# Second attention and expert rounds in one block: the norms of three token chunks in the attention's tail, the fourth within the first expert steps

## The chip, the cores and the metric

One NeuronCore of a Trainium2 chip runs the whole program in one launch. The metric is the device time of one execution in microseconds (us); lower is better. The engines are PE (TensorE, matmuls), DVE (VectorE), ACT (ScalarE), POOL (GpSimd) and SP (SyncE, which here only issues transfers). Each runs its own list of instructions in order and waits for the others through semaphores.

## What is computed

Two layers over 2 x 1024 tokens of 128 channels. The first (a rotary attention and a windowed transformer) is not touched. The second, cut to what matters here:

```python
h = causal_attention(norm(x))          # 16 heads of 8 channels, scores over 1024 tokens
h = layernorm(h_in + z) * gamma + beta # z: the heads' output, NaN taken as 0
x = x + g2 * h
cur = adaln(x)                         # layer norm, scale and shift by the condition
for r in range(4):                     # expert rounds
    w = top2_softmax(cur @ Wg[r] + bg[r])                # 4 experts, 2 kept
    cur = cur + sum_e w[e] * (gelu(cur @ W1[e] + b1[e]) @ W2[e] + b2[e])
x = x + g5 * cur
```

## The kernel before

Activations lie with channels on the partitions, tokens along the free dimension, in four **chunks** of 512 tokens. `causal_block` runs the second attention, then `heads_and_experts` runs everything behind it, each in a block of its own: at the end of a block all engines meet, and the semaphores are cleared.

**Second attention** (`attention`, L661 on). Eight units `it` (four heads of one batch each) of 16 **quarters** give `LAST` = 128 quarters `g`. In each quarter PE computes four score tiles (`score`, L835) into three PSUM banks, ACT turns each into probabilities with Exp (L925), and PE adds the values of the quarter before (`values`, L853, L856, L862). A score tile waits until ACT has emptied the bank of three tiles before. Besides, PE runs 11 quarters ahead with matmuls (L803) whose row maxima DVE reduces (L936), so that DVE has no maxima to reduce in the last 11 quarters. POOL multiplies the diagonal probabilities by a triangle (`mask`, L1020) in eight quarters of each unit, four and four. At a unit's end ACT copies the sums out of PSUM (`take_sums`, L911), PE transposes them (`turn`, L825), DVE divides (L955, L960) and SP stores the heads to DRAM (`store_z`, L761). What else is due in a quarter is listed by `entries(g)`, and PE works it off behind `values(g - 1)`.

**Heads and norms** (`heads_and_experts`, L1793 on). SP loads the heads back as rows of 128 channels (L1885), then the expert weights and small tables (L1886 to L1892). For each chunk: DVE's `compare` and `guard` (L2127, L2133) take NaN as 0, PE transposes (`turn`, L1916), DVE adds to `h` (L2138). Then follow two norms of class `ChunkNorm`, n3 and n4: PE averages over channels (L331), DVE subtracts (L336), ACT squares (L341), PE sums the squares (`variance`, L347), ACT takes the root (L353), DVE inverts (L358), PE spreads the inverse over the partitions (L364), DVE rescales (L370), ACT adds the shift (L375); between the norms DVE adds to x (`add_x`, L2142). The four chunks go through this as a pipeline of `PERIODS` = 8 written out by hand. POOL meanwhile splits both weight tensors into a high and a low part (L2099, L2102, L69), since every product of the experts is made of three matmuls (L74, L75, L76).

**Expert steps.** `STEPS` = 64 steps n, 16 a round: chunk n // 4 % 4, expert n % 4. A step is `up(n)` (12 matmuls), `activate(n)` on ACT (four Gelu, L2033, three copies, L2039), `cast_first` and `lower_hidden` on DVE (L64, L69), `lower_last` on POOL (L2094), `down(n)` (12 matmuls), `weigh(n)` on DVE (L2169) and `add_term` on POOL (L2089). PE issues `up(n + 1)` ahead of `down(n)`.

**Gates.** Each half of the tokens in each round has a gate g: `gate_logits` on PE (L1965), ranking on DVE (L2192 to L2221), `gate_exp` (L2044), `turn_weights` (L1971), `take_rows` (L2024), then SP stores the rows (L1898) and loads them spread over the partitions (L1904), which `weigh` of its eight steps waits for. `gate_after` places the parts: logits behind step 8g - 7, the turning in step 8g - 2, rows behind `activate(8g - 1)`. `weigh(0)` stands on DVE behind `cast_first(2)`.

```python
                for n in range(1, STEPS):
                    if n + 1 < STEPS:
                        up(n + 1)
                    if n == 1:
                        turn_weights(0)
                    g = gate_after(n - 5)
                    if g:
                        turn_weights(g)
                    down(n)
                    g = gate_after(n)
                    if g:
                        gate_logits(g)
```

## Time and profile before

| | us |
|---|---|
| three runs | 1779.31, 1780.4, 1783.44 |
| median | 1780.4 |
| the profiled execution | 1784.86 |
| its span in the trace | 1783.1 |
| PE busy in the span | 1555.6 (87%) |
| DVE busy | 1349.5 (76%) |
| ACT busy | 1193.9 (67%) |
| POOL busy | 623.2 (35%) |

The span starts with the first instruction and ends with the last; the profiled execution took 1.8 us more than its span and 4.5 us more than the median. The granted clock is a share of TensorE's 2.4 GHz: 1.00 is 2.4 GHz, 0.50 is 1.2 GHz. A row of the timeline gives the start and the duration of an instruction or of a merged run of equal ones (x4), the engine, the line, and in square brackets how long the engine had been idle before it and what released it.

### The profile page before, as it was taken

To read this page: it belongs to the slowest core of one execution; us is meant where nothing else is said; L and a number is where in the kernel's file an instruction comes from. 1 tells how busy PE (TensorE), PEld (TensorE's weight loads), DVE (VectorE), ACT (ScalarE), POOL (GpSimd) and SP (SyncE) were. 2 spreads that over 40 slices of the span, in tenths; PEclk is the share of its full clock that TensorE was granted. 3 is DMA by queue.
4 is the path that set the end of the run, shared out by engine and by line. 5 is a ranking of instruction groups with operands and counts; after the bars stand their busy time and mean duration, and the time that the engine had idled before them with its cause. 6 is when DMAs were issued, how large, how long until landed. Compare 5 with 4: busy or idle time off the path is not lost. (4 is left out here: it accounts for less than half of the span.)

```text
span 1783.1 us, 29420 instructions
## 1 busy us (share of the span) xinstructions
PE 1555.6 (87%) x11136; PEld 856.1 (48%) x11136; DVE 1349.5 (76%) x1876; ACT 1193.9 (67%) x2314; POOL 623.2 (35%) x510
## 2 busy tenths in 40 slices
PE   6699999996589886898985999999966799999998
PEld 4122222222457663576641233333324688878886
DVE  3799999981777456775446999999915499999996
ACT  4368888885377742777551787788763577787776
POOL 2710000000577542775230122222213255555554
PEclk9689999998599987999995899999997799999999
DMA  2320110001011100111003201110011111111111
GB/s 75 106 89 20 31 24 19 1 2 51 25 31 31 50 1 18 31 31 31 4 20 94 90 20 28 32 26 6 5 19 60 35 50 43 48 43 48 43 47 53
DMA packets 68284, 66.05 MB, mean 37 GB/s; under 512 B 40840, under 2 KB 44296, under 8 KB 67632
## 3 DMA queue, kind: packets, MB, share of 16 engines
q1 hardware_dynamic: 67504, 61.94, 13.1%
q8 instruction: 89, 1.46, 0.3%
q10 hardware_dynamic: 576, 2.16, 0.3%
q14 instruction: 51, 0.42, 0.1%
q0 software_dynamic: 64, 0.07, 0.0%
HBM read 40.85 MB, written 14.81 MB: 31 GB/s over the span
## 5 line engine op out<-in xcount | busy, mean ns | idle before, releaser
L936 DVE TENSOR_REDUCE att_neg_max<-psum 128x1 f32<-128x1024 f32 x512 | 600.6, 1218 | 46.8 <-PE psum L803 42.6
L925 ACT ACTIVATE att_probs<-psum 128x512 f32<-128x512 f32 x1024 | 532.3, 604 | 142.4 <-PE psum L835 139.9
L803 PE MATMUL psum<-att_k_op,att_q_op 48*128 48x512 bf16 x1024 | 339.2, 406 | 20.3 <-DVE att_neg_max L936 11.9
L835 PE MATMUL psum<-att_q_op,att_k_op 50*128 50x512 bf16 x1024 | 314.3, 387 | 25.2 <-ACT att_probs L925 25.1
L2033 ACT ACTIVATE moe_hidden<-psum,moe_b 128x512 f32<-128x512 f32 x256 | 167.4, 690 | 83.5 <-PE psum L76 83.3
L835 PEld LDWEIGHTS psum<-att_q_op,att_k_op 50*128 50x128 bf16 x1024 | 78.0, 94 | 272.7 <-ACT att_probs L925 218.3
L69 DVE TENSOR_TENSOR moe_hidden_low<-moe_hidden,moe_hidden_high 128x512 fp32r<-128x512 f32 x192 | 203.8, 1108 | 5.4 <-ACT moe_hidden_high L2039 5.3
L853 PE MATMUL psum<-att_probs,att_v 128*32 128x512 f32 (+2 forms) x1664 | 203.2, 558 | 2.9 <-ACT att_sums L911 2.8
L1020 POOL TENSOR_TENSOR att_diag<-att_probs,att_triangle 128x512 f32<-128x512 f32 x64 | 81.0, 1266 | 278.0 <-PE psum L856 172.6
L2094 POOL TENSOR_TENSOR moe_hidden_low<-moe_hidden,moe_hidden_high 128x512 fp32r<-128x512 f32 x64 | 93.6, 1462 | 169.7 <-ACT moe_hidden_high L2039 169.7
L803 PEld LDWEIGHTS psum<-att_k_op,att_q_op 48*128 48x128 bf16 x1024 | 73.7, 95 | 126.1 <-DVE att_neg_max L936 101.5
L1684 POOL TENSOR_TENSOR wl_qk<-wl_qk,wl_part 128x512 f32<-128x512 f32 x64 | 81.5, 1274 | 106.7 <-DVE wl_part L1563 106.7
L2089 POOL TENSOR_TENSOR moe_cur<-moe_cur,moe_term 128x512 f32<-128x512 f32 x64 | 105.8, 1652 | 14.0 <-DVE moe_term L2169 13.8
L74 PE MATMUL psum<-moe_hidden_high,moe_w_high 128*128 128x512 f32 x256 | 103.5, 404 | 5.6 <-DVE moe_hidden_low L69 5.6
L2039 ACT ACTIVATE moe_hidden_high<-moe_hidden 128x512 fp32r<-128x512 f32 x192 | 106.6, 625 | 0.0
L74 PE MATMUL psum<-moe_cur_high,moe_w_high 128*128 128x512 f32 x256 | 101.9, 398 | 0.0
L1580 DVE TENSOR_REDUCE wl_mx<-psum 128x4 f32<-128x512 f32 x64 | 44.0, 687 | 75.6 <-PE psum L1296 75.6
L76 PE MATMUL psum<-moe_hidden_high,moe_w_low 128*128 128x512 f32 x256 | 100.8, 394 | 0.0
L75 PE MATMUL psum<-moe_hidden_low,moe_w_high 128*128 128x512 f32 x256 | 100.8, 394 | 0.0
L76 PE MATMUL psum<-moe_cur_high,moe_w_low 128*128 128x512 f32 x256 | 100.2, 391 | 0.0
L75 PE MATMUL psum<-moe_cur_low,moe_w_high 128*128 128x512 f32 x256 | 100.1, 391 | 0.0
L1009 POOL COPY att_v<-v_tok 128x256 f32<-128x256 f32 x16 | 6.4, 400 | 248.6 <-PE psum L853 246.3
(254 smaller groups left out, 2851.5 us busy)
## 6 DMA issues: line engine op xcount, KB each, us to landing
moe_spread_weights<-gate_rows SPq DMA_DIRECT2D x64, 256.0 KB, 3.2
wl_v_shift<-wl_v SPq DMA_DIRECT2D x62, 128.0 KB, 2.2
att_q_op<-qk_parts SPq DMA_DIRECT2D x32, 192.0 KB, 3.3
att_k_op<-qk_parts SPq DMA_DIRECT2D x32, 192.0 KB, 4.3
qk_parts<-att_hi SPq DMA_DIRECT2D x12, 256.0 KB, 4.0
qk_parts<-att_hi SPq DMA_DIRECT2D x12, 192.0 KB, 2.9
att_q_op<-att_neg_rows SPq DMA_DIRECT2D x128, 2.0 KB
qk_parts<-att_mid SPq DMA_DIRECT2D x8, 256.0 KB, 3.2
```

Of the source, the lines that this page charges most:

```text
L69: return dve.tensor_tensor(dst, src, high.bitcast(F32), ALU.subtract)
L74: pe.matmul(out, w_high, x_high, start=start, stop=False)
L75: pe.matmul(out, w_high, x_low, start=False, stop=False)
L76: return pe.matmul(out, w_low, x_high, start=False, stop=stop)
L803: mm = pe.matmul(buf[:, half * CHUNK:(half + 1) * CHUNK], q_op[it % RING][at_rows(p, MAX_ROW), j, t * P:(t + 1) * P], k_op[it % RING][at_r ...
L835: pe.matmul(st_bank[e % 3], k_op[it % RING][at_rows(p, MAX_ROW + 2), j, t * P:(t + 1) * P], q_op[it % RING][at_rows(p, MAX_ROW + 2), j, ha ...
L853: last = pe.matmul(out[:, 0:full], stage_v[r][:, t, j, :], pr[:, 0:full], start=first_tile, stop=final and full == CHUNK, skip_group_check ...
L925: act.activation(probs[:, g % PB, h, :], st_bank[e % 3], ACT.Exp, scale=scale).then_inc(exp_done, 1)
L936: dve.tensor_reduce(neg[:, t, 2 * p + j:2 * p + j + 1], ring[e % 2], AX.X, ALU.max, negate=True).then_inc(ring_free, 1)
L2033: act.activation(hidden[:, n % 2, f, :], k.psum[:, f, :], ACT.Gelu_apprx_tanh, bias=b1[:, e, f:f + 1]).then_inc(gelu_done, 1)
L2039: act.activation(hidden_high[:, n % 2, f, :], hidden[:, n % 2, f, :], ACT.Copy)\
L2089: pool.tensor_tensor(cur[:, at], cur[:, at], term[:, n % 2, :], ALU.add).then_inc(added, 1)
```

## The change

The two blocks become one: `heads_and_experts` is called from `attention` and gives it pieces that each engine runs inside and behind the attention's own work. What it does:

- SP loads the weights behind the operands of unit 3, in unit 0, and the heads of chunks 0 to 2 in units 3, 5 and 7; those of chunk 3 behind the last store. There are four semaphores `z_stored`, one a chunk.
- POOL splits the weights in units 1 and 2, and clears `square` in unit 3, each behind the fourth mask.
- In the last ten quarters PE, ACT and DVE work off the transposing, n3, `add_x` and n4 up to the variance for chunks 0 to 2 (`tail_on_pe`, `tail_on_act`, `tail_on_dve`). The squares and the shifts of both norms move from ACT to DVE (`square_on_dve`, `add_shift_on_dve`).
- Behind the last `turn` follow n4's rescaling of chunks 0 to 2 and gate 0. Chunk 3 goes through its heads and both norms within steps 0 to 5; gate 1 (its logits need chunk 3) moves from step 1 to step 6, its turning from step 6 to step 8, its rows from behind `activate(7)` to behind `activate(9)`.
- `take_rows(0)` moves into `activate(3)`, `down(2)` waits for it, and `weigh(0)` stands behind `lower_hidden(2)`.
- `cur` takes the memory of `v_ch`, the raw weights that of `centred_x` and `square`; other tensors lie where the attention's were. The banks of the norms are 5, 6, 4, 6, and the last turn takes banks 0 and 1.

In the diff, the order is: the new pieces of `ChunkNorm`; `attention` on SP, PE, ACT, DVE and POOL; the placing of the gates; then the work in the tail and behind it on PE, ACT, POOL and DVE.

```diff
+    def square_on_dve(self, dve, c):
+        dve.wait_ge(self.centred, c + 1)
+        d = self.d[:, self.at[c]]
+        dve.tensor_tensor(self.sq[:, self.at[c]], d, d, ALU.mult).then_inc(self.squared, 1)
+    def add_shift_on_dve(self, dve, c):
+        dve.wait_ge(self.scaled, c + 1)
+        dve.tensor_scalar(self.dst[:, self.at[c]], self.d[:, self.at[c]], self.shift(c * CHUNK // SEQ), None, ALU.add)\
+           .then_inc(self.shifted, 1)
 ...
+                if behind and it == 0:
+                    then.load_weights(sp)
                 if causal and it:
                     store_z(it - 1)
+                if behind and it in (3, 5, 7):
+                    then.load_z(sp, it // 2 - 1)
             if causal:
                 store_z(UNITS - 1)
-                sp.wait_ge(z_stored, 16 * GROUP * UNITS)
+            if behind:
+                then.load_z(sp, CHUNKS - 1)
+                then.on_sp(sp)
 ...
                 extras(entries(g))
+                if behind:
+                    then.tail_on_pe(pe, g)
             values(LAST - 1)
+            if behind:
+                then.last_variance(pe)
             turn(UNITS - 1)
+            if behind:
+                then.on_pe(pe)
 ...
+                if behind:
+                    then.tail_on_act(act, g)
 ...
-            work(order[2 * CHUNKS:])
+            work(order[2 * CHUNKS:-1])
+            if behind:
+                then.tail_on_dve(dve)
+            turn(UNITS - 1)
+            if behind:
+                then.on_dve(dve)
 ...
                     for t in range(SEQ_TILES):
                         mask(it, t)
+                        if behind and t == 3:
+                            then.split_weights(pool, it)
 ...
+    def gate_at(n, first, later):
+        if n == first:
+            return 1
+        g = n // 8 + 1
+        return g if n % 8 == later and 2 <= g < GATES else None
 ...
+    banks = [5, 6, 4, 6]
+    OUT_BANKS = (5, 4, 7)
 ...
+    def tail_on_pe(pe, g):
+        left = own.quarters - g
+        if left == 10:
+            turn_z(pe, 0)
+        if left == 9:
+            turn_z(pe, 1)
+            average3(pe, 0)
+        if left == 8:
+            average3(pe, 1)
+            turn_z(pe, 2)
+        if left == 7:
+            n3.variance(pe, 0)
+            n3.variance(pe, 1)
+            average3(pe, 2)
+        if left == 6:
+            n3.variance(pe, 2)
+        if left == 4:
+            n3.spread_inverse(pe, 0)
+            n3.spread_inverse(pe, 1)
+        if left == 3:
+            n3.spread_inverse(pe, 2)
+            average4(pe, 0)
+        if left == 2:
+            average4(pe, 1)
+            average4(pe, 2)
+        if left == 1:
+            n4.variance(pe, 0)
+            n4.variance(pe, 1)
+    def last_variance(pe):
+        n4.variance(pe, 2)
 ...
+                pe.wait_ge(n4.scaled, (1, 3)[n])
+            elif n == 2:
+                pe.wait_ge(rows_done, 1)
 ...
+        for c in range(3):
+            n4.spread_inverse(pe, c)
+        gate_logits(0)
+        up(0)
+        for n in range(STEPS):
+            if n + 1 < STEPS:
+                up(n + 1)
+            if n == 1:
+                average3(pe, 3)
+            if n == 2:
+                turn_weights(0)
+                n3.variance(pe, 3)
+            if n == 3:
+                n3.spread_inverse(pe, 3)
+            if n == 5:
+                n4.spread_inverse(pe, 3)
+            if n == 6:
+                gate_logits(1)
+            g = gate_at(n, 8, 6)
+            if g:
+                turn_weights(g)
+            down(n)
+            if n == 0:
+                turn_z(pe, 3)
+            if n == 3:
+                average4(pe, 3)
+            if n == 4:
+                n4.variance(pe, 3)
+            g = gate_at(n, None, 1)
+            if g:
+                gate_logits(g)
+    def tail_on_act(act, g):
+        if own.quarters - g == 5:
+            for c in range(3):
+                n3.root(act, c)
+        if own.quarters - g == 1:
+            for c in range(3):
+                n4.root(act, c)
 ...
+        act.wait_ge(small_loaded, 16 * 4)
+        activate(0)
+        activate(1)
+        gate_exp(0)
+        for n in range(2, STEPS):
+            activate(n, 0 if n == 3 else None)
+            if n == 3:
+                n3.root(act, 3)
+            if n == 5:
+                n4.root(act, 3)
+            g = gate_at(n, 9, 7)
+            if g:
+                take_rows(g)
+            g = gate_at(n, 8, 4)
+            if g:
+                gate_exp(g)
+    def split_weights(pool, it):
+        if it == 1:
+            for stored in own.stored:
+                pool.wait_ge(stored, 16 * 2 * TERMS)
+            pool.wait_ge(weights_loaded, 16 * 2)
+            pool.tensor_copy(w1_high[:, :, :], w1).then_inc(w1_split, 1)
+            pool.wait_ge(w1_split, 1)
+            low_part(pool, w1_low[:, :, :], w1, w1_high[:, :, :]).then_inc(w_split, 1)
+        if it == 2:
+            pool.tensor_copy(w2_high[:, :, :, :], w2).then_inc(w2_split, 1)
+            pool.wait_ge(w2_split, 1)
+            low_part(pool, w2_low[:, :, :, :], w2, w2_high[:, :, :, :]).then_inc(w_split, 1)
+        if it == 3:
+            pool.wait_ge(w_split, 2)
+            pool.memset(square[:, :], 0.0).then_inc(cleared, 1)
 ...
+    def tail_on_dve(dve):
+        compare(dve, 0)
+        guard(dve, 0)
+        compare(dve, 1)
+        guard(dve, 1)
+        add_head(dve, 0)
+        compare(dve, 2)
+        guard(dve, 2)
+        add_head(dve, 1)
+        deviations(n3, dve, 0)
+        deviations(n3, dve, 1)
+        add_head(dve, 2)
+        deviations(n3, dve, 2)
+        for c in range(3):
+            n3.invert(dve, c)
+        dve.wait_ge(norm_loaded, 16)
+        add_x(dve, 0)
+        add_x(dve, 1)
+        deviations(n4, dve, 0)
+        add_x(dve, 2)
+        deviations(n4, dve, 1)
+        deviations(n4, dve, 2)
+        for c in range(3):
+            n4.invert(dve, c)
 ...
+        current(0)
+        current(1)
+        first_cast(0)
+        current(2)
+        shift_logits(0)
+        first_cast(1)
+        rank_logits(0, 1)
+        cast_first(0)
+        lower_hidden(0)
+        compare(dve, 3)
+        guard(dve, 3)
+        first_cast(2)
+        rank_logits(0, 2)
+        cast_first(1)
+        lower_hidden(1)
+        add_head(dve, 3)
+        rank_logits(0, 3)
+        keep_two(0)
+        normalise(0)
+        deviations(n3, dve, 3)
+        for i in range(1, STEPS + 1):
+            if i + 1 < STEPS:
+                cast_first(i + 1)
+            if i > 1:
+                weigh(i - 1)
+            if i + 1 < STEPS:
+                lower_hidden(i + 1)
+            if i == 1:
+                weigh(0)
+            if i == 2:
+                n3.invert(dve, 3)
+                add_x(dve, 3)
+            if i == 3:
+                deviations(n4, dve, 3)
+            if i == 4:
+                n4.invert(dve, 3)
+            if i == 5:
+                current(3)
+                first_cast(3)
 ...
+            g = gate_at(i, 6, 2)
+            if g:
+                shift_logits(g)
+                rank_logits(g, 1)
+            g = gate_at(i, 7, 3)
+            if g:
+                rank_logits(g, 2)
+                rank_logits(g, 3)
+                keep_two(g)
+            g = gate_at(i, 7, 4)
+            if g:
+                normalise(g)
```

## Rows read from the trace of the kernel before

**Rows 1.** Busy time by stretch: start:end, length, then busy us of each engine (instructions), clock, DMA share, GB/s.

```profile
1200.00:1285.00 85.00, 80.53 (x790) 28.29 (x784) 78.46 (x77) 67.94 (x133) 21.66 (x20) 1.00 0.10 11
...
1337.00:1350.00 13.00, 8.59 (x28) 5.86 (x28) 5.73 (x9) 2.18 (x3) 2.38 (x2) 0.50 0.63 212
...
1396.00:1420.00 24.00, 17.25 (x79) 13.66 (x77) 8.59 (x31) 12.99 (x22) 4.40 (x4) 0.79 0.15 43
...
1487.00:1534.00 47.00, 46.37 (x211) 37.71 (x211) 43.75 (x66) 36.35 (x61) 25.13 (x16) 1.00 0.14 46
```

**Rows 2.** Timeline, end of the attention and start of the block behind it.

```profile
1326.70 0.60 ACT L911 ACTIVATE att_sums<-psum 128x512 f32<-128x512 f32 x1 [1.90 <-PE psum L862]
1328.94 0.42 DVE L960 TENSOR_TENSOR att<-psum,att_rec 128x256 f32<-128x256 f32 x1
...
1337.68 0.69 DVE L2127 TENSOR_TENSOR moe_centred_x<-moe_cur 128x512 f32<-128x512 f32 x1 [8.32 <-DMA moe_cur<-z_heads]
```

**Rows 3.** Timeline of ACT: table load and Gelu of step 0, table load and root.

```profile
1376.11 1.28 ACT L2033 ACT_TABLE_LOAD   x1 [4.83 <-PE psum L76]
1377.40 2.42 ACT L2033 ACTIVATE moe_hidden<-psum,moe_b 128x512 f32<-128x512 f32 x4
...
1383.13 1.28 ACT L353 ACT_TABLE_LOAD   x1
1384.46 0.26 ACT L353 ACTIVATE moe_deviation<-psum,eps 128x4 f32<-128x4 f32 x1
```

**Rows 4.** Timeline of the first gate: rows, their spreading, the first weighing.

```profile
1413.07 0.25 ACT L2024 ACTIVATE moe_weight_rows<-psum 32x128 f32<-32x128 f32 x1
1418.58 0.75 DVE L2169 SCALAR_TENSOR_TENSOR moe_term<-psum,moe_b,moe_spread_weights 128x512 f32<-128x512 f32 x1 [8.15 <-DMA moe_spread_weights<-gate_rows]
```

**Rows 5.** Timeline of PE: the first matmul behind down(6).

```profile
1447.27 0.39 PE L74 MATMUL psum<-moe_cur_high,moe_w_high 128*128 128x512 f32 x1
```

**Rows 6.** Timeline of ACT: exps of a quarter behind a turn, and of a plain quarter.

```profile
1292.50 2.06 ACT L925 ACTIVATE att_probs<-psum 128x512 f32<-128x512 f32 x4 [1.59 <-PE psum L835]
...
1305.29 2.06 ACT L925 ACTIVATE att_probs<-psum 128x512 f32<-128x512 f32 x4 [0.33 <-PE psum L835]
```

**Rows 7.** Timeline of PE at full clock: average, variance, transposing, spreading, average.

```profile
1360.91 1.02 PE L331 MATMUL psum<-h,ones_mean_sb 128*128 128x512 f32 x2
1361.77 0.95 PE L347 MATMUL psum<-ones_mean_sb,moe_square 128*128 128x1 f32 x8
...
1364.29 0.64 PE L1916 MATMUL psum<-ident,moe_square 128*128 128x128 f32 x4
1364.76 1.06 PE L364 MATMUL psum<-ident,moe_inverse 128*128 128x128 f32 x8
1365.65 1.02 PE L331 MATMUL psum<-x_ch,ones_mean_sb 128*128 128x512 f32 x2
```

**Rows 8.** Timeline of DVE: compare under POOL's split, rescaling, subtraction, cast.

```profile
1351.25 3.31 DVE L2127 TENSOR_TENSOR moe_centred_x<-moe_cur 128x512 f32<-128x512 f32 x1
...
1367.61 0.75 DVE L370 SCALAR_TENSOR_TENSOR moe_centred_x<-moe_centred_x,moe_norm_cols,psum 128x512 f32<-128x512 f32 x1 [0.20 <-PE psum L364]
...
1369.07 0.42 DVE L64 CAST moe_cur_high<-moe_cur 128x512 fp32r<-128x512 f32 x1
```

**Rows 9.** Timeline of POOL: a mask of the tail, the split of w1.

```profile
1317.25 1.26 POOL L1020 TENSOR_TENSOR att_diag<-att_probs,att_triangle 128x512 f32<-128x512 f32 x1 [21.34 <-PE psum L856]
...
1349.51 4.51 POOL L69 TENSOR_TENSOR moe_w_low<-moe_w,moe_w_high 128x2048 fp32r<-128x2048 f32 x1
```

**Rows 10.** The line of the maxima: times min/median/max in ns, first and last start.

```profile
L936 DVE TENSOR_REDUCE att_neg_max<-psum x512: 1211/1215/1227, 69.2 to 1296.6; 128x1 f32<-128x1024 f32 x171
```

**Rows 11.** Costliest groups of the page: the low parts on DVE.

```profile
L69 DVE TENSOR_TENSOR moe_hidden_low<-moe_hidden,moe_hidden_high 128x512 fp32r<-128x512 f32 x192 | 203.8, 1108 | 5.4 <-ACT moe_hidden_high L2039 5.3
```

**Rows 12.** DMA issues: the weights, KB each, us to landing.

```profile
moe_w<-in_moe_w SPq DMA_DIRECT2D x2, 1024.0 KB, 8.7
```

**Rows 13.** Timeline of DVE: three low parts without POOL beside them.

```profile
1385.94 1.89 DVE L69 TENSOR_TENSOR moe_hidden_low<-moe_hidden,moe_hidden_high 128x512 fp32r<-128x512 f32 x3
```

852 lines of the change are left out of this document (378 added, 474 removed).

## The prediction

> **What bounds the kernel now.** I read the busy time by stretch first, then the timelines of the engines from 1285 us on. In the attention PE is busy for 80.5 of 85 us and in the settled expert steps for 46.4 of 47, both at full clock [rows 1]. Between the two it is not: in the first 13 us of the new block PE works at half clock, and among the first expert steps the granted clock is 0.79 with 6.8 of 24 us idle [rows 1]. The reader is to see three landmarks. The last values of the attention end at 1326.6, when ACT takes the sums; the divided heads are there at 1329.4, and the first compare starts only at 1337.7, since the heads go to DRAM and back across the end of the block [rows 2]. The first Gelu starts at 1377.4 [rows 3]. The first matmul behind `down(6)` starts at 1447.27 [rows 5]; from there on a round of eight steps takes 47.0 us [rows 1]. A settled step is 24 matmuls at 0.227, 5.44 us, so seven steps need 38 us, and 69.9 pass between the first Gelu and the end of `down(6)`. So 50.8 us lie between attention and first Gelu, and some 30 us of waits and norm work among the first seven steps. The change attacks both.
>
> **What is added to the tail.** Every PE instruction put into a quarter lengthens that quarter by itself: in a plain quarter ACT idles 0.33 before its exps, behind a `turn` (about 1 us of PE) it idles 1.59 [rows 6]. The loop goes score, exp, freed bank, fourth score, values, next score, and has no room on PE. At full clock, start to start, a transposing costs 0.47, a spreading 0.89, an average 0.86, a variance 0.92 to 0.95 [rows 7]. Ahead of the last values stand 3 transposings (1.4), 6 averages (5.2), 5 variances (4.6) and 3 spreadings (2.7): 13.9 us. The roots of n3 stand amid the exps on ACT: a load of Sqrt, one of Exp, 1.28 each, and three roots, some 0.75 [rows 3], less the 0.33 of idle time: 3.0 us, all on the loop. That DVE's division and norms could make PE wait I checked chunk by chunk: 15 operations of about 0.7 (compare [rows 2]; rescaling, cast [rows 8]) up to n3's inverses run beside seven quarters, and DVE has no maxima left there. It is late once, in `add_x(2)` ahead of the third average of n4, where POOL's masks run too: 1 us. The square on DVE I take like a compare, 0.69; the shift has no row, and lies between the cast's 0.42 and the rescaling's 0.75; I take 0.42, being one input and one output in SBUF as the cast. Sum of the tail: 13.9 + 3.0 + 1.0 = 17.9, so the last values end at 1344.5 instead of 1326.6.
>
> A page speaks against those roots amid exps. The rows show that a switch costs a load of 1.28 and 0.05 until the root starts [rows 3]. The Trainium skill, "ScalarE: Activation LUTs", section "What ACT_TABLE_LOAD costs", puts a switch at about 2.66 us with a drain and asks to batch functions by set. By it the tail would cost 2.8 us more and the first Gelu come 1.4 later, and the forecast would be 1751 instead of 1747; the trace shows no such drain.
>
> **From the last values to the first Gelu.** `last_variance` and root 2 stand ahead of the last `take_sums`: 0.9 + 0.4. From there to the divided heads it is 2.7, as before [rows 2]: 1348.5. DVE then rescales and shifts two chunks, 2 x (0.75 + 0.42) with gaps 2.4, casts, 0.4; POOL's low part is 1.3, like a mask of the same shape [rows 9]; the first three matmuls 0.8; then the load of Gelu, which stands behind the wait as it did before, 1.3 [rows 3]. The three spreadings and the logits on PE (4.4) run beside this. First Gelu: 1354.7. **Saved up to there: 22.7.** What hides what was removed: the store and load of the heads of units 0 to 5 now lie beside quarters long before; the loads of the weights, 8.7 us [rows 12], and POOL's splits lie in units 1 and 2, where POOL idles 21 us between its masks of a unit [rows 9] and the splits need 6.4 and 7.3 of it. If that cover were gone, a mask would be late by what is left. SP's seven issues of weights come behind unit 3's operands, at the start of unit 1, whose next maxima rows are due five quarters later; were they late, PE would wait for at most the 8.7 us of the load once. The reductions do not feel POOL: 1211 to 1227 ns through all 512, masks or not [rows 10]. Only chunk 3's heads still pass through DRAM behind the end: divided at 1348.5, some 8.3 us later in SBUF [rows 2], 1356.8, before DVE comes to them at about 1359.
>
> **The first seven steps.** PE needs 2.0 for the rest of `up(0)`, 14 x 2.72 for `up(1)` to `up(7)` and `down(0)` to `down(6)`, 5.8 for chunk 3 (transposing, two averages, two variances, two spreadings), 1.7 for gate 1's logits and 0.3 for a turning, 48 us in all; it is 1.3 ahead at the first Gelu. Its waits, from walking the order of each engine: 0.9 for `guard(3)` behind `lower_hidden(0)`; 2.0 for `add_head(3)`, which stands behind `lower_hidden(1)`; and 4.2 for n3's inverse of chunk 3. That one hangs on gate 0: `take_rows(0)` stands behind the Gelus of step 3, about 1373.8; from rows to weighing it is 5.5 [rows 4], so `weigh(0)` starts at 1379.3, and behind it on DVE are queued `cast_first(3)`, `weigh(1)`, `lower_hidden(3)` and only then the inverse, at 1384, for which PE waits with `spread_inverse(3)` ahead of `down(3)`. In all 48.0 - 1.3 + 7.1 = 53.8 against 69.9. **Saved: 16.1.** `down(6)` ends at about 1408.5.
>
> **What is given back later.** Gate 1 is now short: exps behind `activate(8)`, so PE waits about 1.5 for `weights_ready` ahead of `down(8)`, and its turning adds 0.3. Its rows come behind `activate(9)`, plus 5.5 [rows 4]: `weigh(8)` starts some 5 us late on DVE, but PE only asks for `lower_hidden(10)` a step later; I book 1.5, since DVE, busy 43.8 of 47 [rows 1], catches up slowly. Together 3.3. From step 12 on the order is the old one. For the clock I book 2.0: three waits of 2 to 4 us on PE fall where before, among longer ones, it granted 0.79 [rows 1]. The bound above is half clock for all that stands between 1340 and 1400, some 12 us more.
>
> **Sum.** 22.7 + 16.1 - 3.3 - 2.0 = 33.5. The profiled execution took 1784.9, so one like it would take 1751.4; it lay 4.5 above the median of the runs, 1780.4, so the forecast for the median is **1747**.
>
> **Rivals.**
> *The clock stays low.* If PE is granted 1.2 GHz through gaps at 1340 to 1355 and again through steps 0 to 5, it gives back up to 12 us, with DVE's collisions in the tail 2 more: about 1760. For it speaks that each stall of the old start had it [rows 1]; against it, that the gaps are a third as long. Chance 0.2.
> *The waits dissolve.* Should the 4.2 us wait and the 3.3 given back be hidden by the buffers of two steps, and the clock hold, the time is about 1740. Chance 0.18.
> *Work is only moved.* PE runs in order, so all norm work put into the tail is paid there. Were DVE to fall behind by 1 to 2 us at each of the ten insertions, the tail would grow by 33 instead of 18 and the steps would give half: about 1770. Chance 0.05.
> *Slower: another phase between DVE and POOL.* Three low parts take DVE 1.89 alone [rows 13] and 1.11 each on average with POOL beside them [rows 11]; a compare that met POOL's split took 3.31 instead of 0.69 [rows 8], ending as that split did [rows 9]. If the new start leaves the steps in a phase in which one more operation a step meets POOL, DVE needs about 1.1 more of each: 5.5 + 1.1 = 6.6 a step against 5.9, 0.7 on 56 steps, 39 us, less the 38.8 gained at the start, with the 3.3 and 2.0: about 1786. It decides from 0.6 us a step on. Against it: eight steps took 47.0 us again and again before, with DVE and PE falling into the same places behind every gate. Chance 0.04. The Trainium skill, "SBUF — State Buffer", section "SBUF: two separate sides", says that DVE and POOL share a port pair as an exclusive lock for a whole instruction; by that rule, which the long compare agrees with, such a collision costs the rest of POOL's instruction and no more.
>
> **How the numbers follow.** The forecast has 0.53, and 1741 to 1755 as its own range (the shift at 0.75 adds 1, the clock 0 to 6, the waits of PE 3 either way). The range that holds 8 in 10 reaches into the first two rivals: 1737 to 1762. A measurement of this kernel can tell about 0.2%, 3.6 us. Faster by more than that are all cases but the last and a remainder: 0.94; within it 0.02; slower 0.04.
>
> **What would show it.** In the trace of the changed kernel: exps of the last ten quarters with idle time of 0.33 plus the inserted work; a pair of table loads in the last five quarters and an ACT gap to the last sums of near 3 us; last values near 1344, first Gelu near 1355, end of `down(6)` near 1408; PE waiting for `ln3`'s inverse ahead of `down(3)`; DVE waiting for the spread rows at `weigh(0)` and `weigh(8)`; 47.0 us for eight steps from step 16 on. The forecast is wrong if quarters before 118 or settled steps change in length, or if PE's clock falls below 0.8 over the first six steps.

## The result, and the profile of the changed kernel

The changed kernel takes **1769.8 us** (median of five runs, 1765.85 to 1771.53), beside 1780.4 before (1777.33 to 1783.44): a ratio of 0.9934, 95% interval 0.9914 to 0.9955. On a later occasion it took 1765.9 (1765.34 to 1767.78), 0.9906 (0.9890 to 0.9923). So it is faster, by 10.6 us where 33 were forecast, and its time lies outside the forecast range of 1737 to 1762.

The profiled executions are 15.1 us apart in their spans (1783.1 and 1768.0). Part of that is no effect of the change: its stretch begins behind the last row maxima of the second attention, which DVE has written out (`att_neg_rows`) at 1300.8 before and at 1297.7 after. The two traces are 3.1 us apart already when ACT copies the second attention's first sums (at 1010.58 and 1007.43), and from there on a unit takes 42.6 us in both. Over all the kernels below this moment lies anywhere between 1296.4 and 1301.8. The rows of DVE, before and after:

```profile
1300.54 0.29 DVE L946 TENSOR_TENSOR att_neg_rows<-psum,att_neg_rows 64x128 bf16<-64x128 f32 x1
...
1297.37 0.29 DVE L963 TENSOR_TENSOR att_neg_rows<-psum,att_neg_rows 64x128 bf16<-64x128 f32 x1
```

From here on I count from the end of that instruction:

| us behind the last row maxima | last values end | first Gelu | from there to the first matmul behind `down(6)` | the rest |
|---|---|---|---|---|
| before | 25.8 | 76.6 | 69.9 | 335.8 |
| forecast | 43.7 | 53.9 | 53.8 | 341.1 (3.3 given back, 2.0 for the clock) |
| after | 54.5 | 68.4 | 60.0 | 342.0 |

Two of the stretches are off: 14.5 us up to the first Gelu, 6.2 in the steps. First the busy time by stretch of the changed kernel; the columns are those of [rows 1].

```profile
1282.00:1297.00 15.00, 13.49 (x168) 5.91 (x159) 10.89 (x11) 11.06 (x22) 5.06 (x4) 1.00 0.01 2
...
1304.00:1310.00 6.00, 4.29 (x20) 1.56 (x18) 4.14 (x7) 2.06 (x4) 0.00 (x0) 0.82 0.11 33
1310.00:1319.00 9.00, 8.74 (x30) 4.25 (x27) 1.11 (x2) 2.56 (x5) 0.00 (x0) 0.50 0.00 0
1319.00:1325.00 6.00, 5.74 (x24) 2.34 (x23) 1.38 (x2) 2.07 (x4) 0.00 (x0) 0.50 0.01 3
1325.00:1336.00 11.00, 8.91 (x39) 3.27 (x37) 0.95 (x4) 7.27 (x13) 1.26 (x1) 0.54 0.00 0
1336.00:1347.00 11.00, 9.28 (x68) 3.55 (x67) 10.43 (x14) 4.41 (x9) 2.52 (x2) 1.00 0.00 1
1347.00:1354.00 7.00, 6.37 (x73) 5.04 (x73) 1.16 (x4) 3.82 (x9) 1.26 (x1) 0.88 0.01 2
1354.00:1365.00 11.00, 9.94 (x53) 9.37 (x54) 7.04 (x20) 0.78 (x3) 1.93 (x2) 0.66 0.25 36
1365.00:1385.00 20.00, 17.45 (x67) 13.18 (x66) 17.33 (x31) 15.64 (x25) 5.78 (x5) 0.89 0.00 1
1385.00:1405.00 20.00, 14.68 (x64) 11.75 (x64) 9.73 (x14) 11.16 (x18) 6.87 (x5) 0.83 0.28 80
...
1518.00:1565.00 47.00, 46.39 (x211) 37.63 (x210) 42.57 (x65) 36.34 (x60) 24.97 (x16) 1.00 0.13 46
```

The reader is to see that TensorE is nearly always busy from 1310 to 1325, and still little gets done: it works at half clock (1.2 of 2.4 GHz), inside the attention, where before it had full clock to the last quarter. The forecast had no such stretch there. The timeline of ACT shows what this makes of the quarters:

```profile
1297.34 2.06 ACT L938 ACTIVATE att_probs<-psum 128x512 f32<-128x512 f32 x4 [0.54 <-PE psum L842]
...
1304.15 2.06 ACT L938 ACTIVATE att_probs<-psum 128x512 f32<-128x512 f32 x4 [1.77 <-PE psum L842]
1310.49 0.60 ACT L938 ACTIVATE att_probs<-psum 128x512 f32<-128x512 f32 x1 [4.28 <-PE psum L842]
...
1319.65 2.07 ACT L938 ACTIVATE att_probs<-psum 128x512 f32<-128x512 f32 x4 [6.61 <-PE psum L842]
1325.15 2.06 ACT L938 ACTIVATE att_probs<-psum 128x512 f32<-128x512 f32 x4 [3.43 <-PE psum L842]
1327.23 1.28 ACT L341 ACT_TABLE_LOAD   x1
1328.52 0.57 ACT L341 ACTIVATE moe_deviation<-psum,eps 128x4 f32<-128x4 f32 x3
1329.11 1.28 ACT L938 ACT_TABLE_LOAD   x1
1330.41 2.06 ACT L938 ACTIVATE att_probs<-psum 128x512 f32<-128x512 f32 x4
...
1353.94 0.59 ACT L924 ACTIVATE att_sums<-psum 128x512 f32<-128x512 f32 x1
1364.75 1.28 ACT L2117 ACT_TABLE_LOAD   x1 [10.22 <-PE psum L66]
1366.04 2.42 ACT L2117 ACTIVATE moe_hidden<-psum,moe_b 128x512 f32<-128x512 f32 x4
```

A quarter's exps wait 4.28 and 6.61 us for its scores where [rows 6] had 0.33 and 1.59. The pair of table loads amid the exps costs what was booked: 3.2 us from the end of one quarter's exps to the start of the next (booked were 3.0 beyond the idle time of 0.33). What came between is in the timeline of DVE, with the first weighing further on:

```profile
1305.34 0.69 DVE L2201 TENSOR_TENSOR moe_centred_x<-v_ch 128x512 f32<-128x512 f32 x1 [4.10 <-DMA v_ch<-z_heads]
...
1393.03 0.75 DVE L2283 SCALAR_TENSOR_TENSOR moe_term<-psum,moe_b,moe_spread_weights 128x512 f32<-128x512 f32 x1 [8.14 <-DMA moe_spread_weights<-gate_rows]
...
1394.69 4.44 DVE L59 TENSOR_TENSOR moe_hidden_low<-moe_hidden,moe_hidden_high 128x512 fp32r<-128x512 f32 x3
1399.05 0.17 DVE L346 RECIPROCAL moe_inverse<-moe_deviation 128x4 f32<-128x4 f32 x1
```

and in that of PE, down to the first matmul behind `down(6)`, which answers to [rows 5]:

```profile
1307.42 1.65 PE L319 MATMUL psum<-h,ones_mean_sb 128*128 128x512 f32 x2 [1.24 <-DVE h L2211]
...
1313.59 3.57 PE L335 MATMUL psum<-ones_mean_sb,moe_square 128*128 128x1 f32 x16
...
1399.27 2.07 PE L352 MATMUL psum<-ident,moe_inverse 128*128 128x128 f32 x8 [5.32 <-DVE moe_inverse L346]
...
1425.99 0.39 PE L64 MATMUL psum<-moe_cur_high,moe_w_high 128*128 128x512 f32 x1
...
1436.81 0.41 PE L2060 MATMUL psum<-ident,moe_weight 128*32 128x128 f32 x2 [2.44 <-DVE moe_weight L2335]
```

The timeline of SP's queue around the load of chunk 2's heads:

```profile
1297.70 2.21 SPq L752 DMA_DIRECT2D att_q_op<-att_neg_rows  x4
1299.95 2.33 SPq L761 DMA_DIRECT2D z_heads<-att  x4
1302.32 0.58 SPq L1933 DMA_DIRECT2D v_ch<-z_heads  x1
```

The compare of chunk 2 waits 4.10 us for its heads. `load_z(2)` stands on SP's queue in unit 7, behind the rows of the last queries, which exist only with the last row maxima, and `store_z(6)`; it is issued at 1302.32, and the heads land at 1305.3. PE meets that wait in the average of h (L319), 1.24 us, and that instruction takes 1.65 instead of 1.02 [rows 7]; a spreading of 0.89 to 1.06 there is 2.07 here, behind the wait of 5.32. So there are two questions: what lets the clock fall in the tail, and what the waits among the steps cost with it.

### The profile page after: what moved, and what is told of

It reads as the page before. It is cut to its first block and busy times, and to the rows that moved or that the text cites. A ratio compares the mean times of both kernels' runs of the same rounds, so it can differ in the third digit from the quotient of the medians.

```text
span 1768.0 us, 29416 instructions
## 1 busy us (share of the span) xinstructions
PE 1561.3 (88%) x11136; PEld 856.8 (48%) x11136; DVE 1352.7 (77%) x1892; ACT 1187.9 (67%) x2302; POOL 623.7 (35%) x510
## 5 line engine op out<-in xcount | busy, mean ns | idle before, releaser
L59 DVE TENSOR_TENSOR moe_hidden_low<-moe_hidden,moe_hidden_high 128x512 fp32r<-128x512 f32 x192 | 191.7, 1045 | 8.0 <-ACT moe_hidden_high L2125 7.8
L2176 POOL TENSOR_TENSOR moe_hidden_low<-moe_hidden,moe_hidden_high 128x512 fp32r<-128x512 f32 x64 | 99.0, 1547 | 171.8 <-ACT moe_hidden_high L2125 171.8
L2171 POOL TENSOR_TENSOR v_ch<-v_ch,moe_term 128x512 f32<-128x512 f32 x64 | 101.4, 1585 | 23.1 <-DVE moe_term L2283 22.8
L65 PE MATMUL psum<-moe_hidden_low,moe_w_high 128*128 128x512 f32 x256 | 102.8, 402 | 0.0
L65 PE MATMUL psum<-moe_cur_low,moe_w_high 128*128 128x512 f32 x256 | 100.1, 391 | 0.0
```

The costliest lines, as they stand in the source:

```text
L59: return dve.tensor_tensor(dst, src, high.bitcast(F32), ALU.subtract)
L65: pe.matmul(out, w_high, x_low, start=False, stop=False)
L2171: pool.tensor_tensor(cur[:, at], cur[:, at], term[:, n % 2, :], ALU.add).then_inc(added, 1)
```

## The experiments

Two theories for the tail. T, the trigger: a wait of PE lets the clock fall, and half clock then stretches all behind it. M, the mix: the alternation of short float32 work (averages, variances, transposings) with the waits for the exps lets it fall, load or no load, and more work for PE would hold it. A third is that the overlap of norms and attention is itself worth nothing. Each kernel is the changed one with the edits named; the traces are read with the same marks:

| kernel | time, us (runs) | against before, 95% | last values | first Gelu | to behind `down(6)` | rest |
|---|---|---|---|---|---|---|
| e1 load early | 1760.4 (1759.0 to 1763.8) | 0.9886 (0.9870, 0.9902) | 45.9 | 56.4 | 59.9 | 342.1 |
| e2 heads first | 1764.4 (1758.5 to 1765.8) | 0.9898 (0.9882, 0.9915) | 46.2 | 56.7 | 59.9 | 342.1 |
| e3 norms behind | 1764.2 (1760.4 to 1767.6) | 0.9902 (0.9881, 0.9924) | 25.8 | 62.5 | 60.3 | 342.0 |
| e4 weigh late | 1759.5 (1754.8 to 1764.1) | 0.9879 (0.9856, 0.9901) | 51.9 | 64.6 | 53.2 | 340.1 |
| e5 = e1 + e4 | 1756.8 (1749.0 to 1761.1) | 0.9845 (0.9823, 0.9867) | 50.6 | 64.4 | 54.2 | 341.8 |
| e6 = e3 + e4 | 1757.9 (1756.2 to 1761.1) | 0.9865 (0.9848, 0.9882) | 25.8 | 62.7 | 54.1 | 341.9 |
| e7 = e5 + idle matmuls | 1757.5 (1750.5 to 1758.0) | 0.9851 (0.9831, 0.9872) | 45.9 | 59.8 | 54.3 | 341.7 |
| e8 idle matmuls alone | 1762.5 (1758.2 to 1765.1) | 0.9886 (0.9868, 0.9905) | 48.4 | 60.4 | 59.9 | 342.1 |
| e9 changed kernel again | 1765.9 (1765.3 to 1767.8) | 0.9906 (0.9890, 0.9923) | 52.0 | 65.3 | 58.2 | 342.0 |
| e10 = e5 + turn late | 1750.7 (1746.0 to 1755.4) | 0.9819 (0.9796, 0.9842) | 46.2 | 56.7 | 54.1 | 338.1 |
| e11 = e10 + more idle matmuls | 1749.5 (1746.5 to 1753.3) | 0.9814 (0.9792, 0.9835) | 45.9 | 56.4 | 54.3 | 338.1 |
| e12 = e10, tiles moved | 1752.7 (1750.8 to 1755.9) | 0.9837 (0.9819, 0.9854) | 45.9 | 56.4 | 54.3 | 338.1 |
| e13 = e4 + turn late | 1758.5 (1758.1 to 1759.0) | 0.9877 (0.9861, 0.9893) | 51.9 | 64.8 | 53.2 | 338.1 |
| e14 = e10, hidden shifted | 1753.0 (1751.4 to 1754.1) | 0.9845 (0.9830, 0.9860) | 45.9 | 58.9 | 52.7 | 339.5 |
| e15 = e10 again | 1748.5 (1746.6 to 1751.1) | 0.9821 (0.9807, 0.9836) | 45.9 | 56.4 | 54.4 | 338.1 |

**e1, the load one unit earlier.**

```diff
-                if behind and it in (3, 5, 7):
-                    then.load_z(sp, it // 2 - 1)
+                if behind and it in (3, 5, 6):
+                    then.load_z(sp, {3: 0, 5: 1, 6: 2}[it])
```

> Edit: the heads of chunk 2 are loaded at the end of unit 6 instead of unit 7 (they are complete by then). In the changed kernel DVE waits 4.1 us for them, and PE 1.24 us behind it for h of chunk 1; right behind this the granted clock falls to 0.50 and stays there for some 27 us of the attention's tail. Theory T (trigger): that wait is what drops the clock. Then the clock is 1.00 from quarter 118 to the last values, the tail is shorter by 10 to 12 us, and the kernel takes 1756 to 1761 instead of 1769.8. Rival M (mix): the work put into the tail (variances of one column, float32 transposings, a PE that waits for exps) drops the clock by itself. Then both waits go, the clock falls all the same a little later, and 1 to 3 us are gained: 1767 to 1769.

The first Gelu came at 56.4 instead of 68.4, with the clock at 1.00 until about 1325; the variances that took 3.57 us above took 1.95. That is 12.0 of the 14.5 us, and the time lies where T had it (1756 to 1761). It fits T, since the wait is gone and the clock stays.

**e2, both heads of chunks 0 and 1 added ahead of the compare of chunk 2** (the load stays late).

```diff
         add_head(dve, 0)
+        add_head(dve, 1)
         compare(dve, 2)
         guard(dve, 2)
-        add_head(dve, 1)
```

> Edit: on DVE add_head of chunk 1 stands ahead of compare of chunk 2, so that PE does not wait for h of chunk 1 while the heads of chunk 2 are on their way; the heads still land late. T: PE's first average of chunk 1 starts at once, but the transposing of chunk 2, in the same quarter, then waits for the late heads (about 2 us), so the clock falls as before: within 2 us of 1769.8. Were the clock to hold here and not where the heads come early, it would hang on the order on DVE and not on the wait. M: within 2 us of 1769.8 as well, with the fall of the clock where it was.

With the heads as late as in the changed kernel, PE did not wait for DVE here, and the first Gelu again came at 56.7. In this trace the clock did fall, at 1316.8 and behind no wait over 0.47 us, but only in the quarter ahead of the gap in which ACT loads tables and PE waits anyway, so that it cost next to nothing. Neither theory had this, nor a time 5.4 us under 1769.8. The run was the fastest of its five, and the median is 5.9 us above it, so of the usual execution of this kernel the trace says little: the whole execution had a mean granted clock of 0.937 in the profiled run and of 0.930 or 0.931 in the other four.

**e3, the norms behind the last values** (order alone: PE's norm work of the tail stands behind the loop, and ACT's likewise).

```diff
-                if behind:
-                    then.tail_on_pe(pe, g)
             values(LAST - 1)
             if behind:
+                for g in range(LAST):
+                    then.tail_on_pe(pe, g)
```

> Edit: one part of the change undone: what PE and ACT do for the norms of chunks 0 to 2 in the last ten quarters now stands behind the last values (ACT: behind the last exps); everything else is as in the changed kernel. If overlap in the tail brings what it was put there for, the last values end near 1323 in this kernel's trace, but the norms then run alone, DVE and PE waiting for each other: first Gelu 8 to 15 us later than in the changed kernel, 1778 to 1785 in all. If the tail's half clock eats what overlap brings (PE pays all of it in line anyway), the first Gelu comes within 3 us of the changed kernel's, and the time within 4 us of 1769.8.

Last values at 25.8, as before the change; all the norm work then follows, and the first Gelu comes at 62.5, earlier than in either of the two outcomes that were expected. That is 5.9 us ahead of the changed kernel and 2.8 ahead of its second trace (e9). The time is that of the changed kernel on e9's occasion (0.9902 and 0.9906). So as built, the overlap with the tail brings nothing that these times show. That the low clock takes what it saves is the likely reason; e3's own clock is 0.70 to 0.84 among its norms (1330 to 1361), so the two are not a pair that differs in the overlap alone.

**e4, the first two weighings behind n3's inverse of chunk 3.**

```diff
-            if i > 1:
+            if i > 2:
                 weigh(i - 1)
             if i + 1 < STEPS:
                 lower_hidden(i + 1)
-            if i == 1:
-                weigh(0)
             if i == 2:
                 n3.invert(dve, 3)
+                weigh(0)
+                weigh(1)
                 add_x(dve, 3)
```

> Edit: on DVE the weighing of steps 0 and 1, which waits for the first gate's rows to come back from DRAM (8.1 us of idle DVE), stands behind cast_first(3), lower_hidden(3) and n3's inverse of chunk 3, instead of ahead of them. In the changed kernel PE waits 5.3 us ahead of down(3) for that inverse, and its clock falls for some 3 us. Theory W (this order is the cause): the wait of PE goes, down(3) waits only for weigh(0), at about 1393, and step 3 and all behind it come 4 to 7 us earlier: 1763 to 1766. Rival: PE catches the gap up anyway, since DVE is the slower engine in the steps behind it; then within 1.5 us of 1769.8.

The steps up to `down(6)` take 53.2 instead of 60.0. PE's wait of 5.32 for the inverse is gone, and the spreading behind it takes 1.05 instead of 2.07. The median is 3.5 us under the range of 1763 to 1766 that was expected. One thing more moved, which was not forecast: the rest takes 340.1 instead of 342.0 (see e10).

**e5 (e1 and e4) and e6 (e3 and e4).**

> Edit: e1 (heads of chunk 2 loaded in unit 6) and e4 (weighing of steps 0 and 1 behind lower_hidden(3)) together. The two lie in different stretches, so they should add: e1's trace was 12.0 us shorter up to the first Gelu, e4's 6.7 us shorter from there to the end of down(6) and 1.9 behind it. Expected 1749 to 1753. If 1757 or more, one of the two gains was luck with the clock of that execution.

> Edit: e3 (norms of chunks 0 to 2 on PE and ACT behind the last values) and e4 together: how much the overlap in the attention's tail is worth once the late weighing is mended. In e3 the first Gelu came 62.5 us behind the last row maxima, in e1 56.4, in the changed kernel 68.4. If the tail's overlap is worth its 6 us only where PE does not wait for heads, this kernel takes 1756 to 1759, 5 to 7 more than e5. If it is worth nothing, within 2 us of e5.

The gain of e4 in the steps is there in both (54.2, 54.1). But e5's trace is the surprise of the study. Its instructions up to the first Gelu are e1's, PE does not wait for heads, and still the clock falls, in the variances of chunks 0 and 1 of n3 (L335), which take 2.90 us instead of 1.95. It is the very instruction in which it falls in e4, e9 and e13, where the load is late (2.35, 2.60 and 2.41). That instruction, then busy time by stretch of e5:

```profile
1311.53 2.90 PE L335 MATMUL psum<-ones_mean_sb,moe_square 128*128 128x1 f32 x16
...
1309.00:1319.00 10.00, 9.07 (x42) 3.95 (x39) 2.91 (x5) 4.62 (x9) 0.00 (x0) 0.66 0.00 0
1319.00:1325.00 6.00, 5.74 (x28) 2.21 (x20) 0.00 (x0) 2.57 (x5) 0.00 (x0) 0.50 0.01 3
1325.00:1335.00 10.00, 7.70 (x36) 3.46 (x32) 2.51 (x7) 5.60 (x11) 1.27 (x1) 0.61 0.00 0
```

The first Gelu is at 64.4, eight us behind e1's. T as the only cause falls: the clock can fall without a late load, in one execution and not in another, and e5's runs, 12 us apart, are the widest of all. The profiled execution is the slowest of the five. The time is over the 1749 to 1753 expected of two gains that add. And e6, which has no overlap, is 1.1 us from it, with overlapping intervals. Where the clock stays, the overlap is worth some 6 us (first Gelu 56.4 in e1 against 62.5 and 62.7 in e3 and e6); e6 with the turning of e10 was not run, so what the overlap is worth in the end is not shown.

**e7 and e8, idle matmuls to keep the clock up** (two bf16 matmuls of 512 columns per quarter into a free bank, in e5 and in the changed kernel).

```diff
                     score(g, i)
+                    if behind and i == 2 and g > LAST - 10:
+                        for _ in range(2):
+                            pe.matmul(k.psum[:, 3, :], k_op[it % RING][at_rows(0, MAX_ROW + 2), 0, 0:P],
+                                      q_op[it % RING][at_rows(0, MAX_ROW + 2), 0, 0:CHUNK], start=True, stop=True)
```

> Edit: e5, and in each of the last nine quarters two bf16 matmuls of 512 columns, whose result nobody reads, in the 0.47 us in which PE waits for the first exp. They raise PE's activity and should cost no time there. M (the mix of work drops the clock, even without a wait: in e2 it fell at quarter 123 with PE never waiting over 0.5 us) expects 1.00 from quarter 118 to the last values in this trace and 2 to 4 us less than e5. If only long waits drop the clock, it still falls once in the 3.4 us gap behind the roots of n3, and the time is e5's within 1.5 us.

> Edit: the changed kernel with the same two idle bf16 matmuls a quarter, and with the heads of chunk 2 still late. T (the wait of 1.24 us is the trigger) expects the clock to fall in quarter 120 all the same; but with more activity behind it it should rise again within a few quarters, where in the changed kernel it took ten: 1762 to 1766. If activity alone decides, the clock does not fall at all, and the time is e1's, 1758 to 1761.

e7 has e5's time; its clock holds until the gap of the table loads, nearly as M wanted, but the 2 to 4 us did not come. e8 seemed to gain, 0.9886 against 0.9934, but the control made later puts the changed kernel at 0.9906, and that interval overlaps e8's. PE's wait of 1.25 us for h was there, and its trace kept 0.83 to 1.00 in the tail where the changed kernel's had 0.50: the clock fell at 1314 and was back at 1317, soon, as T expected with idle matmuls. With one trace of each, a gain of idle work is not shown.

**e9, the changed kernel once more**, beside e10 to e12.

> The changed kernel as it is, beside the next three on one chip. Both theories: 1768 to 1771 us, its own median being 1769.8; first Gelu 68 us behind the last row maxima of the second attention, 60 us from there to the first matmul behind down(6). If it comes out near 1763 instead, the chip of the earlier runs, and not their edits, carried a part of what they gained, and every gain over the changed kernel has to be read against this run.

It came out between the two cases: 3.9 us under its own first median. Differences of that size between kernels timed on different occasions mean nothing; e1 to e8 are therefore read by their traces, and by times only within e1 to e4 and within e5 to e8, each timed together.

**e10, `turn_weights(1)` behind `down(8)`.**

```diff
             g = gate_at(n, 8, 6)
-            if g:
+            if g and n != 8:
                 turn_weights(g)
             down(n)
+            if n == 8:
+                turn_weights(1)
```

> The kernel with the early load and the early weighing of tokens, and with the turning of the second half's weights put behind down(8) instead of ahead of it. If down(8) waits for the weights' row and the clock falls behind that wait, TensorE's wait of 2.4 us there goes, and the half clock of the 3 us behind it with it: 2 to 4 us less than the 1756.8 of the kernel with both edits, 1753 to 1755, and the stretch from the first matmul behind down(6) to the end 338 to 339.5 us instead of 341.8. Rival: weigh(8) and the sums behind it were late anyway, so the wait only moves to the next down step: the stretch stays at 341 to 342 and the time at 1756 to 1757.

The rest takes 338.1 instead of 341.8, the wait and the half clock behind it are gone, and the 3.7 us are there. How they divide, e4 and e5 show. The turning of the second half's weights, PE, first e4 and then e5:

```profile
1424.07 0.41 PE L2060 MATMUL psum<-ident,moe_weight 128*32 128x128 f32 x2 [2.14 <-DVE moe_weight L2335]
...
1428.02 0.41 PE L2060 MATMUL psum<-ident,moe_weight 128*32 128x128 f32 x2 [2.13 <-DVE moe_weight L2335]
```

Both wait as long, with the same instructions behind. In e4 the clock stays at 1.00 (1423 to 1430), in e5 it is 0.76 (1427 to 1434), and the rest takes 340.1 and 341.8. So the wait is worth 2.0 (e4 to e13, 340.1 to 338.1) and the clock 1.7, which came in one execution and not in the other. The median fell by 6.1 where 3.7 is explained; the two were timed on different occasions, and this trace had its first Gelu at 56.7: with e5 it makes a pair of equal instructions in the tail, 7.7 us apart.

**e11, more idle matmuls** (e10 with two in each of eight quarters, fourteen in the gap behind n3's roots, four ahead of the last turn; 34 in all).

> The kernel of e10_turn_late with idle matmuls: two per quarter over the last ten quarters, fourteen in the gap in which TensorE waits for the roots of chunk 2, four ahead of the last turn. If it is the mix of short float32 work and waits that lets the clock fall, it stays at 1.00 from the last row maxima to the last turn in every run: first Gelu 54 to 56 us behind the last row maxima (the prediction's own sum gives 53.9), time 1746 to 1750, and its runs lie closer together than those of the other kernels. If the clock falls for a cause outside the kernel, the windows show it below 1.00 all the same, and the time is that of e10 plus what the idle matmuls take in line, 3 us or more.

First Gelu at 56.4, time as e10, and the runs no closer together (6.9 us). The clock showed 0.83 in 1315 to 1325 all the same: it fell behind the gap of the table loads, as in e1, though the fourteen matmuls filled that gap and PE waited 0.54 us there instead of 3.35. Neither the gain nor the loss of 3 us came. M is right that the fall needs no late load (e5), but that more work for PE holds the clock gets no support; nor do the idle matmuls cost anything that can be measured.

**e13 and e15, the load alone, on one occasion.** e13 is e10 with the load of chunk 2 back in unit 7; e15 is e10 unchanged.

> The kernel with the late weighing and the late turning, but with chunk 2's heads loaded in unit 7 again, as the change has it. If the late load and the low clock behind it cost what the traces show between kernels with and without it (first Gelu 60.4 to 68.4 us behind the last row maxima in all four with the late load, 56.4 to 56.7 in five of the seven with the early one), the first Gelu comes 60 us or later and the time is 4 to 8 us above the 1750.6 of e10_turn_late: 1755 to 1759. Rival: the clock falls as it will whatever the load does, and the load costs its own wait of TensorE, 1.2 us: 1751 to 1753.

> The kernel of e10_turn_late unchanged, beside the other two on one chip: 1749 to 1753, first Gelu 56 to 58 us behind the last row maxima. If it comes out as high as e13_load_late_again, the late load costs nothing that can be measured; if its first Gelu lies at 60 or later, the low clock comes without the late load as well.

(The expectation of e13 counts e2 among the kernels with the early load; its load was late.) Of the pair, e13 came out where the late load was expected to put it, and not at the rival's 1751 to 1753. 1758.5 against 1748.5: 9.9 us, and no run of the one overlaps a run of the other. The two profiled executions have their last row maxima at 1300.48 and 1300.53, so their times can be laid side by side. Busy time by stretch, first e13:

```profile
1305.00:1315.00 10.00, 7.59 (x46) 2.82 (x42) 5.17 (x8) 4.82 (x10) 0.00 (x0) 1.00 0.19 33
1315.00:1325.00 10.00, 9.74 (x38) 4.50 (x37) 1.38 (x2) 2.26 (x5) 0.00 (x0) 0.54 0.01 2
1325.00:1335.00 10.00, 7.91 (x31) 2.61 (x31) 0.48 (x3) 7.07 (x13) 1.27 (x1) 0.50 0.00 0
```

then e15:

```profile
1305.00:1315.00 10.00, 8.86 (x57) 4.10 (x53) 4.55 (x7) 4.87 (x10) 0.00 (x0) 1.00 0.10 7
1315.00:1325.00 10.00, 6.40 (x38) 2.09 (x37) 1.87 (x5) 7.24 (x13) 0.00 (x0) 1.00 0.01 2
1325.00:1335.00 10.00, 8.84 (x55) 4.66 (x55) 4.95 (x6) 4.16 (x9) 2.53 (x2) 0.83 0.00 1
```

and the timeline of PE in e13, at the wait and behind it:

```profile
1310.27 1.12 PE L319 MATMUL psum<-h,ones_mean_sb 128*128 128x512 f32 x2 [1.27 <-DVE h L2213]
...
1314.41 2.41 PE L335 MATMUL psum<-ones_mean_sb,moe_square 128*128 128x1 f32 x16
1316.69 2.06 PE L319 MATMUL psum<-h,ones_mean_sb 128*128 128x512 f32 x2
```

PE waits 1.27 us for h; some six us on, the clock is halved, the average takes 2.06 instead of 1.12, and the first Gelu comes 8.4 us later than in e15. The steps give 1.2 back (53.2 against 54.4), so the two profiled executions are 7.1 us apart; e15's was the slowest of its four. The wait itself is an eighth of the 9.9. Nor is 9.9 what the edit is always worth: against the kernel before it is 0.56% here (0.9877 to 0.9821), 0.34% from e4 to e5, and 0.20% to 0.48% from the changed kernel (0.9906, 0.9934) to e1, so from some 4 to 10 us.

Each execution also has its mean granted clock on record, which reaches beyond the one traced execution. It is 0.928 to 0.932 in all nine of the changed kernel (with e9) and 0.931 or 0.932 in e13, but 0.929 to 0.937 in e4, whose load is late too. With the early load it is 0.938 to 0.943 in e15, 0.932 to 0.940 in e10, 0.930 to 0.938 in e1 and 0.930 to 0.940 in e5. (It counts the steps too, where e4's edit takes a stretch of low clock away, so it is to be compared within a kernel or between kernels that differ in the load alone.)

All five kernels with the late load and the changed order (after, e4, e8, e9, e13) have it at 60.4 to 68.4; of the eight with the early load five have 56.4 to 56.7, and e14, e7 and e5 have 58.9, 59.8 and 64.4. So T holds in a weaker form: with the late load the clock falls in the tail in nearly every execution, and without it now and then. Whether PE's wait of 1.2 us is what does it is not shown; e2 has the late load without that wait, and its four untraced executions have the low mean clock. What decides stays open.

**e12 and e14, the hidden tiles elsewhere.** The settled steps became slower by 0.2 us in eight. Matmuls of the stretch 1450 to 1740, by shape, of the kernel before:

```profile
L74 PE MATMUL psum<-moe_hidden_high,moe_w_high 128*128 128x512 f32 x200 | 80.0, 400 | 3.9 <-DVE moe_hidden_low L69 3.9
L75 PE MATMUL psum<-moe_hidden_low,moe_w_high 128*128 128x512 f32 x200 | 78.0, 390 | 0.0
L76 PE MATMUL psum<-moe_hidden_high,moe_w_low 128*128 128x512 f32 x199 | 77.6, 390 | 0.0
```

and of the changed one:

```profile
L66 PE MATMUL psum<-moe_hidden_high,moe_w_low 128*128 128x512 f32 x198 | 78.6, 397 | 0.0
L64 PE MATMUL psum<-moe_hidden_high,moe_w_high 128*128 128x512 f32 x198 | 78.4, 396 | 3.6 <-DVE moe_hidden_low L59 3.6
L65 PE MATMUL psum<-moe_hidden_low,moe_w_high 128*128 128x512 f32 x198 | 78.4, 396 | 0.0
...
L66 PE MATMUL psum<-moe_cur_high,moe_w_low 128*128 128x512 f32 x199 | 77.5, 389 | 0.0
```

Two of the three kinds of down matmul changed, from 390 to 396 and 397 ns; the same instructions, on tiles at other addresses. The third kind (hidden_high with w_high) has in its mean the matmuls behind a wait, which take 500 ns, and cannot be read so closely: 400 before, 396 after. The up matmuls stayed at 389 to 392.

```diff
 # e12
+    spread_w = sb("spread_weights", [P, SPREADS, CHUNK])
     hidden = sb("hidden", [P, 2, FF_TILES, CHUNK])
...
-    spread_w = sb("spread_weights", [P, SPREADS, CHUNK])
 # e14
+    over("pad", 1664)
     hidden = sb("hidden", [P, 2, FF_TILES, CHUNK])
...
-    spread_w = sb("spread_weights", [P, SPREADS, CHUNK])
-    over("max", 1024)
+    over("rest", 8192 - 1664 + 1024)
     term = sb("term", [P, 2, CHUNK])
+    spread_w = sb("spread_weights", [P, SPREADS, CHUNK])
```

> The kernel of e10_turn_late with the tile of spread weights allocated ahead of the hidden tiles, which gives these other addresses in the SBUF and changes no instruction. If the place of the tiles makes the hidden matmuls of the down steps take 396 to 397 ns instead of 390, they take 390 again, eight settled steps take 47.0 us instead of 47.2, and the whole is 1 to 2 us less than e10. Otherwise both stay as in e10, and the difference of the down matmuls has another cause.

> The kernel of e10_turn_late with the three hidden tiles 1664 bytes further on in the SBUF, which puts them back to the distance from multiples of 2048 bytes that they had before the change; no instruction changes. If that distance makes the hidden matmuls of the down steps take 396 to 397 ns, they take 390 again and eight settled steps 47.0 us instead of 47.2. Otherwise 396 to 397 and 47.2 stay, and addresses of the hidden tiles are not the cause.

e12 left all at 396 and 397. e14 changed the pattern, but not to the old one: 393 and 395 for the two kinds, 402 for the one with the waits in it, the up matmuls at 395, 393 and 390, eight settled steps at 47.4, and the rest 1.4 us longer. Neither of the two outcomes that were expected of it came. The place of the tiles moved there (hidden tiles, term and spread weights) does have an effect on these durations; which place gives the old ones was not found, nor that it is this which made 390 into 396. Other placements, of the weights above all, were not tried.

## Why the forecast was wrong

**Right.** The direction, and the parts of the mechanism. The tail's order is the one described. Hiding the weights' load and the splits in units 1 and 2 cost nothing: the splits ran 1.89 and 4.53 us long between POOL's masks, and the unit's period did not change. The table loads cost 1.28 each, with no drain. The Trainium skill, "ScalarE: Activation LUTs", section "What ACT_TABLE_LOAD costs", has a drain with every switch, and by its figure the pair would have taken 2.8 us more, an estimate; this trace does not show it. Where the clock fell only at the gap of the table loads (e1, e15), the forecast stretches came nearly true: last values at 45.9 against 43.7, last values to first Gelu 10.5 against 10.2. Most of the 2.2 us of the first is that fall: behind the gap, values take 1.93 instead of 1.07 and two spreadings 2.74, of which some 0.7 is the clock; 1.6 in all, an estimate from these rows. The settled steps, whose change in length was named as a sign of a wrong forecast, did change, by 0.2 us in eight.

**Wrong, first step: the heads in the tail.** "The store and load of the heads of units 0 to 5 now lie beside quarters long before" was put down without a time. For chunk 2 it is false. The load is queued on SP behind the last unit's rows and `store_z(6)`, and it lands 4.1 us behind the moment at which DVE asks for it. I checked DVE's load chunk by chunk, but not SP's queue for this item.

**Wrong, second step, and most of the miss: the term for the clock.** "For the clock I book 2.0", with half clock expected at most "between 1340 and 1400". It was at 0.50 to 0.54 from 1310 to 1336, inside the quarters, where every instruction of PE lies on the loop. Adding each stretch's length times what the clock lacked gives 18 us up to the first Gelu, and that is too much, since low clock in the gap of the table loads is free: e10 had 0.50 there from 1322 to 1328, and its first Gelu came 0.3 behind e15's. The early load moved the first Gelu by 12.0 between traces, and by 8.4 in the pair e13 and e15. In the steps the same sum is 5.6 us (0.11 of 20 and 0.17 of 20), nearly the whole 6.2 by which that stretch missed. The early load does not always bring this: e4 and e5 have their first Gelu at 64.6 and 64.4, for in e5 the clock fell without a late load. So the term that failed is the clock; that the late load is its usual occasion is shown by e13 and e15, and what makes the clock fall is not.

**Mis-sized: the waits among the steps.** "4.2 for n3's inverse" was right in place and cause; it measured 5.32, with `lower_hidden(3)` at 4.44 beside two sums and two low parts of POOL. `add_head(3)` cost 2.48 against 2.0, and the 0.9 for `guard(3)` did not come. The waits are 7.8 against 7.1, 0.7 us off; the clock, at 0.89 and 0.83, has the other 5.5. In e4 the same stretch took 53.2 with the wait taken away: the forecast's 53.8 was reached, but by another order of DVE's work.

**Mis-sized: what is given back.** In place of 3.3 it is 6.2, made up so: steps 7 and 8 take 15.6 us instead of 10.9, which is 4.7. Of that, PE's wait ahead of `down(8)` is 2.4, for which 1.5 was booked; the turning is 0.3, as booked; most of the rest is the clock, 1.7 by e4 and e5, and some 0.3 stays open. The other 1.4 are the slower settled steps, 0.2 in eight, for which nothing was booked. `weigh(8)`, for which 1.5 stood in the sum, never made PE wait.

**The rivals.** "The clock stays low" was the nearest, right in kind and too small, for it was bounded at 12 us and placed behind the tail. "Work is only moved" (1770) gives the measured number by a mechanism that did not occur: DVE fell behind once, not ten times. With the three repairs (load, weighing, turning: e10, e11, e15) the kernel takes 1748.5 to 1750.7, 0.9821 (0.9807 to 0.9836) in e15. That is the size of the 33 us forecast, by another order of work than the one forecast. That version beats both kernels.

## What to carry over

When work is put into a loop in which one engine runs without slack, list for every moved item the queue that feeds it, DMA queues included, with the time at which it lands; one load that was 4.1 us late cost 4 to 10 us. Price a loop that gets a new mix of work and waits with a term for half clock, and give that term a range: here it came in one execution of the same instructions and not in another. And time a repair beside its control on the same occasion: the changed kernel alone moved by 3.9 us between two.
